# A causal-attention block with mixture-of-LoRA FFN on one core: units in another order, maxima spread by deadline, and the products with values in pairs

## The reference

```python
qkv = x @ W_qkv.T + b_qkv                       # 16 heads of 16
logits = einsum('bhqd,bhkd->bhqk', q, k) / sqrt(16)
logits = where(causal, logits, -inf)            # causal, 2048 x 2048 per head
attn = softmax(logits)
o = einsum('bhqk,bhkd->bhqd', attn, v)          # then W_out, b_out
h = relu(mole(x, W1, b1, A1, B1, R1))           # 256 -> 1024, mixture of 3 LoRA experts
y = mole(h, W2, b2, A2, B2, R2)                 # 1024 -> 256
```

## Time and profile before

| | us |
|---|---|
| median of 3 runs | 1570.16 |
| runs, lowest to highest | 1563.66 to 1574.16 |
| profiled execution, its own time | 1573.55 |
| its span in the trace | 1571.8 |
| PE busy | 1330.6 (85%) |
| DVE busy | 917.3 (58%) |
| ACT busy | 790.8 (50%) |
| POOL busy | 387.8 (25%) |

### The profile page before, as it was taken

The page is one execution under the profiler, slowest core; times in us unless marked ns, Lnnn a source line. Parts: engine busy times, 40 slices in busy tenths (PEclk is TensorE's granted clock), DMA queues, the critical chain, the costliest instruction groups (busy, mean ns, idle before and its releaser), DMA issues. The chain is left out here.

```text
span 1571.8 us, 26356 instructions
## 1 busy us (share of the span) xinstructions
PE 1330.6 (85%) x10096; PEld 763.3 (49%) x10096; DVE 917.3 (58%) x1886; ACT 790.8 (50%) x1193; POOL 387.8 (25%) x534
## 2 busy tenths in 40 slices
PE   4567988899998898999967999899988999899646
PEld 3543443555544444555543555455544545455145
DVE  6446566666767567774245566677776576673023
ACT  2523554446664356665742655356654455555521
POOL 4400122213222013321201322133422123221041
PEclk8757597779998789998985779699998799899868
DMA  5343234022331121320233233124132121210100
GB/s 163 114 132 82 53 100 118 28 55 64 93 103 37 29 66 45 98 88 15 83 106 75 67 107 96 36 59 118 45 92 58 35 59 39 58 34 8 36 21 14
DMA packets 85943, 107.22 MB, mean 68 GB/s; under 512 B 11306, under 2 KB 59378, under 8 KB 85820
## 3 DMA queue, kind: packets, MB, share of 16 engines
q1 hardware_dynamic: 85820, 105.54, 24.3%
HBM read 66.97 MB, written 38.01 MB: 67 GB/s over the span
## 5 line engine op out<-in xcount | busy, mean ns | idle before, releaser
L948 DVE TENSOR_REDUCE mx<-ps 128x1 f32<-128x512 f32 (+3 forms) x1152 | 707.0, 655 | 371.8 <-PE ps L636 182.0
L810 ACT ACTIVATE prob<-ps 128x1024 f32<-128x1024 f32 (+3 forms) x640 | 553.4, 901 | 424.0 <-PE ps L606 211.6
L628 PE MATMUL ps<-kst,qst 48*128 48x512 f32 (+3 forms) x1280 | 322.0, 498 | 122.5 <-DVE mx L948 98.7
L665 PE MATMUL ps<-prob,vw 128*17 128x512 f32 (+3 forms) x2560 | 336.2, 602 | 0.1
L628 PEld LDWEIGHTS ps<-kst,qst 48*128 48x128 f32 x1280 | 145.3, 212 | 380.5 <-issue 281.5
L601 PE MATMUL ps<-qst,kst 50*128 50x512 f32 (+3 forms) x1280 | 300.5, 461 | 8.2 <-ACT prob L810 7.8
L601 PEld LDWEIGHTS ps<-qst,kst 50*128 50x128 f32 x1280 | 139.8, 209 | 82.6 <-ACT prob L810 41.7
L474 POOL TENSOR_TENSOR hid_lo<-hidf,hid_hi 128x512 fp32r<-128x512 f32 x56 | 71.6, 1278 | 338.0 <-ACT hid_hi L899 338.0
L898 ACT ACTIVATE hidf<-ps 128x512 f32<-128x512 f32 x64 | 38.2, 597 | 120.0 <-PE ps L750 115.0
L636 PE MATMUL ps<-mask_q,pick 64*128 64x128 bf16 x1024 | 86.2, 250 | 0.0
L665 PEld LDWEIGHTS ps<-prob,vw 128*17 128x17 f32 x2560 | 43.9, 98 | 86.8 <-issue 60.7
(11 more groups left out here) (157 smaller groups left out, 1703.8 us busy)
## 6 DMA issues: line engine op xcount, KB each, us to landing
kst<-k_rows SPq DMA_DIRECT2D x160, 192.0 KB, 4.1
qst<-q_rows SPq DMA_DIRECT2D x64, 192.0 KB, 4.0
o_rows<-o_sb SPq DMA_DIRECT2D x32, 256.0 KB, 2.0
q_rows<-s_hi SPq DMA_DIRECT2D x56, 128.0 KB
k_rows<-s_hi SPq DMA_DIRECT2D x56, 128.0 KB
sx<-in_x SPq DMA_DIRECT2D x16, 256.0 KB, 4.3
fo<-o_rows SPq DMA_DIRECT2D x32, 128.0 KB
fd<-r_rows SPq DMA_DIRECT2D x32, 128.0 KB
```

The costliest lines, as they stand in the source:

```text
L628: last = pe.matmul(ps[:, M_BANK + banks[a], at:at + width], qst[half, u % Q_BUFS, p, i * P:(i + 1) * P], kst[half, K_SLOT[u, c], p, 0:widt ...
L665: last = pe.matmul(ps[32 * h:32 * h + HD + 1, O_BANK, skip:BLK], vw[:, (NJ * b + t // 4) % V_BUFS, t % 4, g * GH + h, :], prob[:, s % P_BU ...
L810: act.activation(prob[:, s % P_BUFS, 2 * p:2 * p + 2, 0:width], ps[:, bank:bank + 2, 0:width], ACT.Exp).then_inc(a_free, 1)
L948: dve.tensor_reduce(mx[:, u % 2, a, both, i, c], ps[:, M_BANK + bank, 0:n * width].rearrange("p (h x) -> p h x", h=n), AX, ALU.max).then_i ...
```

## The change

Four things are changed.

1. **Order of units.** The four units (0, 3, g) of batch 0's last block, 16 steps each, are no longer followed by the four units (1, 0, g) of batch 1's first block, 4 steps each, but alternate with them: steps 96 to 176 hold 16, 4, 16, 4, 16, 4, 16, 4 steps.
2. **Maxima by deadline.** `pair_steps` no longer spreads a unit's pairs over the unit ahead. It walks the steps, works out in each the rate at which all later pairs must come to meet their deadlines (three steps ahead of their unit), and places that many, if their data are stored and their buffers free by then. Steps 16 to 300 again hold 532 pairs: 240 steps have two (175 of these with a product, 65 without), 20 none, 16 one, 9 four. Before step 0 stand 15 pairs, not 11.
3. **Values in pairs.** `values` of a step no longer stands in every step between `logits(s, 1)` and the second pair. In odd steps, right behind `logits(s, 0)`, the values of the two steps s-3 and s-2 come together; even steps have none.
4. **Job tables.** `S_START`, `F_START`, `D_START` and `SPLIT_STEP` get new numbers, and two waits use the unit that is now the last of its block. Steps 16 to 300 hold 205 products in place of 210, steps 301 to 319 nine in place of five, steps 0 to 15 three in place of one.

```diff
+UNITS = [(0, J, g) for J in range(NJ - 1) for g in range(NG)]
+UNITS += [unit for g in range(NG) for unit in ((0, NJ - 1, g), (1, 0, g))]
+UNITS += [(1, J, g) for J in range(1, NJ) for g in range(NG)]
...
-S_START = [-30, -26, -22, -18, 12, 20, 56, 64, 110, 120, 144, 152, 172, 180, 212, 226]
+S_START = [-26, -22, -15, -7, 10, 20, 48, 56, 64, 74, 112, 126, 172, 180, 212, 226]
...
 def pair_steps():
 
     at = {s: [] for s in range(BEGIN - 1, END)}
-    for u in range(NU):
-        end = FIRST[u] - MAX_LEAD
-        begin = FIRST[u - 1] - MAX_LEAD if u else end - 4
-        for k in range(len(PAIRS[u])):
-            at[begin + k * (end - begin) // len(PAIRS[u])].append((u, k))
+    todo = []
+    for u, (b, J, _) in enumerate(UNITS):
+        for k, pair in enumerate(PAIRS[u]):
+            free = [stored(b, J), stored(b, pair[0]), keys_free(K_BLOCKS.index((u, pair[0]))) + 2]
+            free += [FIRST[u - Q_BUFS + 1] + 2] if u >= Q_BUFS else []
+            todo.append((max(free), FIRST[u] - MAX_LEAD, u, k))
+    begin, owed = stored(0, 0), 0.0
+    todo = collections.deque(todo)
+    for s in range(begin, NSTEP):
+        due, rate = 0, 0.0
+        for n, (_, end, _, _) in enumerate(todo):
+            rate = max(rate, (n + 1) / (end - s))
+            due += end == s + 1
+        owed = min(owed + rate, 4.5)
+        made = 0
+        while todo and todo[0][0] <= s and made < max(due, int(owed + 1e-9)):
+            free, end, u, k = todo.popleft()
+            at[s].append((u, k))
+            made += 1
+        owed = max(0.0, owed - made)
...
                     if 0 <= s < NSTEP:
                         logits(s, 0)
+                    if s % 2:
+                        for done in (s - PV_LAG - 1, s - PV_LAG):
+                            if 0 <= done < NSTEP:
+                                values(done)
                     if s in TURN_AT:
                         turn_maxima(TURN_AT[s])
                     for u, k in first:
                         maximum(u, k)
                     if 0 <= s < NSTEP:
                         logits(s, 1)
-                    if 0 <= s - PV_LAG < NSTEP:
-                        values(s - PV_LAG)
                     for u, k in second:
                         maximum(u, k)
```

More of the change, by code:

```diff
@@ L1 @@
+import collections
 from contextlib import ExitStack
@@ L31 @@
 GH = 4
-UNITS = [(b, J, g) for b in range(B) for J in range(NJ) for g in range(NH // GH)]
+NG = NH // GH
+UNITS = [(0, J, g) for J in range(NJ - 1) for g in range(NG)]
+UNITS += [unit for g in range(NG) for unit in ((0, NJ - 1, g), (1, 0, g))]
+UNITS += [(1, J, g) for J in range(1, NJ) for g in range(NG)]
 NU = len(UNITS)
@@ L35 @@
 NSTEP = FIRST[-1]
+LAST_UNIT = [max(u for u, (b, J, _) in enumerate(UNITS) if NJ * b + J == c) for c in range(NCHUNK)]
+DONE = [FIRST[u + 1] for u in LAST_UNIT]
 STEP = [(u, t) for u, (_, J, _) in enumerate(UNITS) for t in range(4 * (J + 1))]
@@ L49 @@
 A_SLOTS, M_BANK, M_BANKS, O_BANK = 2, 4, 3, 7
-S_START = [-30, -26, -22, -18, 12, 20, 56, 64, 110, 120, 144, 152, 172, 180, 212, 226]
-F_START = [25, 38, 57, 73, 105, 121, 169, 184, 200, 215, 230, 246, 264, 280, 327, 328]
-D_START = [FIRST[NH // GH * (c + 1)] + 3 for c in range(NCHUNK)]
+S_START = [-26, -22, -15, -7, 10, 20, 48, 56, 64, 74, 112, 126, 172, 180, 212, 226]
+F_START = [28, 48, 64, 84, 122, 146, 186, 198, 210, 222, 234, 246, 268, 282, 327, 328]
+D_START = [done + (5 if done < NSTEP else 3) for done in DONE]
 S_CHAIN = [("s_load", 0), ("s_stat", 1), ("s_xhat", 1), ("s_turn", 1), ("s_qk0", 2), ("s_qk1", 1), ("s_v", 1),
@@ L67 @@
 EARLY, LATE = 4, NBLK - 2
-SPLIT_STEP = -16
+SPLIT_STEP = -21
 def place():
@@ L91 @@
 BEGIN, END = min(S_START) - 1, max(WHEN.values()) + 3
+assert all(WHEN["f_load", n] > WHEN["d_store", n // 2] for n in range(NBLK))
 def job_steps():
@@ L116, with keys_free, stored @@
 PAIRS = [unit_pairs(u) for u in range(NU)]
+K_BLOCKS = [(u, c) for u, (_, J, _) in enumerate(UNITS) for c in range(J + 1)]
+K_SLOT = {block: kb % K_BUFS for kb, block in enumerate(K_BLOCKS)}
+K_ROUND = {block: kb // K_BUFS for kb, block in enumerate(K_BLOCKS)}
+def keys_free(kb):
+    if kb < K_BUFS:
+        return BEGIN
+    u, c = K_BLOCKS[kb - K_BUFS]
+    return FIRST[u] + 4 * c + 4
+def stored(b, c):
+    return WHEN["s_store", 2 * (NJ * b + c) + 1] + LOAD_LEAD + 1
 def pair_steps():
     at = {s: [] for s in range(BEGIN - 1, END)}
-    for u in range(NU):
-        end = FIRST[u] - MAX_LEAD
-        begin = FIRST[u - 1] - MAX_LEAD if u else end - 4
-        for k in range(len(PAIRS[u])):
-            at[begin + k * (end - begin) // len(PAIRS[u])].append((u, k))
+    todo = []
[15 more added lines that the diff above has]
+            free, end, u, k = todo.popleft()
+            assert s < end, (u, k, s, end)
+            at[s].append((u, k))
+            made += 1
+        owed = max(0.0, owed - made)
+    assert not todo
     return at
@@ L168, in key_loads @@
 def key_loads():
-    blocks = [(u, c) for u, (_, J, _) in enumerate(UNITS) for c in range(J + 1)]
     at = {s: [] for s in range(BEGIN - 1, END)}
-    for kb, (u, c) in enumerate(blocks):
+    for kb, (u, c) in enumerate(K_BLOCKS):
         need = min(STEP_OF_PAIR[u, k] for k, pair in enumerate(PAIRS[u]) if pair[0] == c)
[L174 to L178, removed]
+        step = max(need - LOAD_LEAD, keys_free(kb))
         b, J, _ = UNITS[u]
@@ L181, in key_loads @@
         at[step].append(kb)
[L182 to L187, removed]
+    return at
+K_LOADS_AT = key_loads()
 def query_loads():
@@ L535, in d_load @@
                 def d_load(c):
-                    sp.wait_ge(o_stored, 16 * NH // GH * (c + 1))
+                    sp.wait_ge(o_stored, 16 * (LAST_UNIT[c] + 1))
                     if c:
@@ L1012, in s_v @@
                     if c >= V_BUFS:
-                        dve.wait_ge(pv_done, FIRST[16 * ((c - V_BUFS) // NJ + 1)])
+                        dve.wait_ge(pv_done, max(DONE[c0] for c0 in range(NCHUNK) if c0 // NJ == (c - V_BUFS) // NJ))
                     bank, free = job_full("s_v", n)
```

## The result

The changed kernel takes 1757.99 us (median of 3 runs, 1738.85 to 1765.67) against 1570.16: 1.114 times, 95% interval 1.097 to 1.131. The forecast was 1572 with a range up to 1650. The ratio leaves out the profiled execution as a slow run (1765.67 us, span 1763.9) and is that of the means of the others, 1748.4 against 1569.3.

The account below looks back on a forecast made before the run. PE was taken to set the time, waiting for DVE's reduces and partly running at 1.2 GHz. 1573.55 - 100 (levelling) + 100 (pairing) - 4 + 6 = 1575.5, less 3.4 for the median: 1572 us, range 1488 to 1650.

Parts of the forecast that it names:

- the waits: PE's waits of maximum pairs for DVE's reduces were to grow from 98.7 to some 150 to 200 us.
- the pair of values: Values of two steps together in odd steps were to take PE 1.84 us, 0.98 plus an estimated 0.86.
- first pair to product: The stretch from a step's first pair to its product was to take 1.80 us in even and odd steps.
- 110 + 18: Cost of pairing: +110 us for 175 product steps and +18 us for 65 light steps.
- Levelling, -100: Unit order and maxima by deadline were to save 100 us in steps 16 to 300, between 0 and 157.
- 205 x 4.29 + 71 x 2.77 + 9 x 2.12 = 1095, x 1.052: Steps 16 to 300 with values unmoved: product, light and pairless steps at full-clock rates, times a dip factor, 1152 us.
- Values in pairs, +100: Pairing takes the cover between a step's two pairs and was to cost 100 us, bounds -44 and +172.
- some tenth disappears in stretches at 1.2 GHz: Pairing's +113 us was cut to +100, since PE is the slower partner at low clock.
- The slower rival: The clock stays at a mean of 0.88 in steps 16 to 300, levelling saves some 20 us: 1637 us, chance 0.21.
- The faster rival: The clock stays full without crowded steps, so the factor of 1.052 goes, 57 us: 1515 us, chance 0.35.
- The drain of a change of tiling mode: Pairing halves the changes to the values' strips; by this alone an estimated 0.24 us per two steps, -29 us in all.
- Head and end, -4 and +6: Before step 0, earlier loads against added pairs and products: -4 us; steps 301 to 319, four more products: +6 us.

Follow-up runs that it names:

- unpaired kernel: Changed kernel with one step's values in every step, back between the second logits and the second pair: 1591.7 us, 1.019 to before.
- the repeated logits: Changed kernel with second logits computed twice in steps with pairs, even, odd or both: 1729.7, 1722.2 and 1709.5 us.
- the shorter reduces: DVE reduces half of each stretch of maxima: changed kernel 1593.1, before 1461.4, unpaired kernel 1497.6 us; a quarter: changed 1560.3, unpaired 1457.8 us.

## Why the prediction was wrong

The 192 us between the profiled executions split so: levelling, with order and tables, +4 in steps 16 to 300 (-100 forecast), pairing +155 there (+100), and everything outside these steps +33 (+2).

**Right:** what bounds (PE, held by the ring of three banks and DVE's reduces), the waits (150 to 200 us forecast, 195.0 measured), the pair of values (1.84), first pair to product, and with them the price of pairing at full clock: 110 + 18 forecast for the 240 steps with two pairs, 109 in the table above. One reading was off without harm: 0.655 us is the mean of a reduce over all widths, and one of 512 columns takes 0.685.

**Levelling, -100, failed.** The step "205 x 4.29 + 71 x 2.77 + 9 x 2.12 = 1095, x 1.052" took its rates from stretches that ran at full clock and a factor from one that nearly did. Alone, levelling measured 0.998, and with order and tables steps 16 to 300 took 1256 us (unpaired kernel), a factor of 1.15. Of the 161 us over 1095 the sum's factor had 57. The clock in the steps with two pairs took 79 (table above), their rates at full clock 31 (962 against 931 by 4.29 and 2.77), and the nine steps with four pairs, which the sum counted as two, most of the rest: 76 us where it had 33. That the one-pair steps before were cheap was left out, too.

**Values in pairs, +100, failed by size and by one step.** It measured 149 to 166 on the changed kernel and 201 on the old one. The step that failed is "some tenth disappears in stretches at 1.2 GHz": the clock was taken as a discount, and it was a second cost. Against the unpaired kernel, idle time in steps 16 to 300 grew by 82 us (210 against 128), which the forecast had, and PE's busy time by 73 with the same instructions, which it had not. The "lost cover" explains the first: the single values at the new place bring 72. Of the second 54 come only with the grouping, which makes odd steps full and even ones thin: it lowers the clock at either place, and the new place alone does not. In the changed kernel the 41 even steps with two pairs and no product took 2.68 us with 0.83 idle, 69% busy; with single values 3.52 with 0.74, 79%. That the thin stretches are what draws the clock is not shown step by step: it rests on the repeated logits, which raised it, and on the rows around 1384.

**The slower rival** had the mechanism and the sign: the clock not above 0.89 decides, and it was 0.83. Its price, 65 us, was too small because it let the clock stay at 0.88, where it fell, and still gave levelling 20 us. The faster rival, with the clock full, is out.

**The drain of a change of tiling mode** (the Trainium skill, TensorEngine Tiling (Array Packing), Tiling Modes, Key Properties), which spoke for pairing, is worth little here: the pair of values took 1.84 us against 0.98 for one, so at most some 0.12 us is saved for two steps, half of the 0.24 that the forecast estimated from no row, and the sum moved the other way. The 320 waits on three banks agree with the rule on repeated gaps (the Trainium skill, Perfetto Trace Analysis, Identifying Performance Opportunities, Optimization Strategy). No run gave the ring a fourth bank; the shorter reduces show only that its reader binds.

**Head and end, -4 and +6.** The loads did move, and the first pair ran at 76.53 in place of 89.40. But the pairs that followed stood alone and waited for their reduces, and the added products came behind them: the first exponential came at 113.32, not 109.58. Steps 0 to 15 took 10 us more. Steps 301 to 319 took 17 more, with four products more and a clock of 0.88 in place of 1.00 (8 more in the unpaired kernel, at 0.97); before they were

```profile
1433.21:1477.38 44.17, 42.07 (x344) 18.86 (x342) 3.67 (x14) 33.52 (x44) 5.28 (x5) 1.00 0.04 14
```

## What to carry to other kernels

Where a matmul engine waits on a reader in a short ring of banks, other work between two fills of the ring is the cover; before moving it, count what is left between each two fills. Ask also how evenly the change lays the engine's work: gaps spread over all steps cost their own time here (72 us more of them, and the same clock), while work in blocks with thin steps between cost that and the clock. So price such a change at both clock levels. A rate from a stretch at full clock holds only for stretches that keep it, and it is well to count how many steps do.

## What was not expected of the hardware

PE did more in the same busy time: 912 matmuls more in steps 16 to 300 left it at 1205 us against 1201, since the granted clock rose from 0.83 to 0.88. With idle time alike (201 and 210 us in the stretch), the clock was 0.89 or 0.83 by whether the values stood in every step or in every second, and over the span it was 0.848 to 0.861 or 0.806 to 0.827 in all runs. A reduce's time falls less than its width: groups of at most 512, 256 and 128 columns took 656, 405 and 278 ns on average (the means hold the narrower forms, too).
